# Attention and mixture-of-experts block: the heads' sums through DRAM instead of a TensorE selection product

## The reference

```
x = x + cross_attention(layernorm(x), ctx, ctx, lengths)   # 8 heads of 16 rows
x = x + moe(layernorm(x))                                  # 8 experts, top 2, gated SiLU

attention, per batch and head (16 rows q, k = v, 512 columns each):
    p   = softmax(s * q^T k)          # over the 512 keys
    out = v p^T                       # 16 rows x 512 queries
```

## Time and profile before

| | |
|---|---|
| median of 3 runs | 1163.27 us (1161.13 to 1163.48) |
| profiled execution | 1159.15 us, span 1157.6 us |
| PE busy | 1032.1 us (89%) |
| DVE busy | 684.7 us (59%) |
| ACT busy | 427.0 us (37%) |
| POOL busy | 629.3 us (54%) |
| attention slots with all parts running | about 77 to 499 us of the span |

### The profile page before, as it was taken

One profiled execution on the slowest core, in us unless ns is written; L12 is line 12 of the kernel. 1 busy time (PEld: TensorE's weight loads), 2 busy tenths in 40 slices (PEclk: granted clock), 3 DMA queues, 4 the chain that ended last, 5 costly groups with the idle time before them and its releaser, 6 DMA issues.

```text
span 1157.6 us, 19040 instructions
## 1 busy us (share of the span) xinstructions
PE 1032.1 (89%) x5098; PEld 413.6 (36%) x5099; DVE 684.7 (59%) x1029; ACT 427.0 (37%) x751; POOL 629.3 (54%) x603
## 2 busy tenths in 40 slices
PE   2899999999999999833999999999999999999970
PEld 0223333333333333211444444444444444444430
DVE  5877777777777777114556545455564555534345
ACT  8277777777777777721111111101011110111110
POOL 5455666666666652321677618348381574800575
PEclk9999999999999999976999999999999999999995
DMA  6575666656665542104878737647585576743779
GB/s 181 184 223 174 187 191 194 190 188 190 193 191 187 176 150 71 45 29 119 236 187 214 227 86 218 174 111 206 147 228 160 149 192 167 200 91 74 158 197 281
DMA packets 213752, 195.86 MB, mean 169 GB/s; under 512 B 138400, under 2 KB 177312, under 8 KB 208288
## 3 DMA queue, kind: packets, MB, share of 16 engines
q1 hardware_dynamic: 198784, 122.27, 40.0%
q0 software_dynamic: 14336, 71.87, 18.8%
q10 hardware_dynamic: 576, 1.05, 0.3%
HBM read 111.48 MB, written 53.00 MB: 142 GB/s over the span
## 4 chain that ended last, share of the span: by engine, by line
PE 77%; DVE 10%; DMA 5%; issue 4%; ACT 1%; POOL 1%; POOLq 1%; SPq 0%; DVEq 0%
PE rows L1169 32%; PE heads_out L1169 16%; PE heads_out L1083 8%; PE scores L1070 8%; DVE nm L768 8%; PE rows L1056 7%; PE misc L1133 2%; PE misc L1110 1%; ACT W L650 1%; DVE st L878 1%; PE misc L1125 1%; DMA sums_dram<-U 1%; PE misc L1103 1%; DMA slots_dram<-cv 0%; PE misc L1149 0%
## 5 line engine op out<-in xcount | busy, mean ns | idle before, releaser
L1169 PE MATMUL rows<-W,U 128*128 (+1 forms) x1776 | 391.5, 380 | 18.3 <-DMA U<-stage 16.9
L768 DVE TENSOR_REDUCE nm<-rows 128x2 f32<-128x1024 f32 x256 | 305.1, 1215 | 80.9 <-PE rows L1056 72.6
L650 ACT ACTIVATE W<-scores 128x512 f32<-128x512 f32 x512 | 284.0, 596 | 124.9 <-PE scores L1070 123.6
L1169 PEld LDWEIGHTS rows<-W,U 128*128 128x128 bf16 x1776 | 174.2, 98 | 229.6 <-issue 22.4
L715 ACT ACTIVATE U<-rows 128x512 f32<-128x512 f32 x78 | 46.3, 597 | 507.8 <-PE rows L1169 492.1
L1169 PE MATMUL heads_out<-W,U 128*128 x888 | 199.4, 381 | 3.3 <-DMA U<-U 3.3
L974 DVE TENSOR_TENSOR U<-rows,U 128x512 bf16<-128x512 f32 x78 | 53.9, 691 | 228.6 <-ACT U L715 228.4
L1056 PE MATMUL rows<-W,U 96*128 96x512 bf16 x512 | 148.5, 400 | 36.3 <-DMA W<-parts_dram 22.5
L434 POOL TENSOR_TENSOR W<-U,W 128x2048 bf16<-128x2048 f32 x42 | 171.4, 4080 | 7.7 <-POOL W L433 7.7
L1070 PE MATMUL scores<-U,W 128*128 128x512 bf16 x512 | 167.7, 384 | 5.9 <-ACT W L650 5.2
L433 POOL TENSOR_SCALAR W<-U 128x2048 bf16<-128x2048 f32 x42 | 80.8, 1924 | 147.0 <-PE rows L1169 139.9
(11 more groups left out here) (169 smaller groups left out, 689.3 us busy)
## 6 DMA issues: line engine op xcount, KB each, us to landing
U<-wpack_dram POOLq DMA_DIRECT2D x42, 1024.0 KB, 5.9
parts_dram<-U SPq DMA_DIRECT2D x32, 384.0 KB, 4.4
U<-parts_dram SPq DMA_DIRECT2D x64, 192.0 KB, 3.4
W<-parts_dram SPq DMA_DIRECT2D x64, 192.0 KB, 4.3
stage<-slots_dram SPq DMA_DIRECT2D x39, 257.0 KB, 3.0
expert_out_dram<-U SPq DMA_DIRECT2D x39, 256.0 KB
parts_dram<-U SPq DMA_DIRECT2D x32, 256.0 KB, 4.4
stage<-wpack_dram POOLq DMA_DIRECT2D x12, 512.0 KB, 4.7
```

What stands on the lines that cost most here:

```text
L650: s.activation(probs[:, w % 2, j, kk, :], sc[u % 2][:, :], ACT.Exp) \
L768: v.tensor_reduce(nm[:, bb.parity, 2 * k:2 * k + 2], p1[k % 2][:, :].rearrange("p (c k) -> p c k", c=2), AX_X, ALU.max, negate=True).then_ ...
L1169: ins = m.matmul(bank, part_of(s_part, k), W[:, bass.ds(at_w, 512)], start=(k == 0 and n == 0), stop=(k == n_chunks - 1 and n == 2))
```

## The change

The two selection products, the matrices `selu`, and ACT's copy of their result go. Instead all 128 rows of each `og` group are stored to `heads_dram`: group 0 by SP in the batch's own slot, after the load of `rb` and before the store of the maxima; group 1 in the next slot, where the sums were stored. `den` is read from the rows of sums in `heads_dram`, and `us` is loaded by one DMA that picks the 16 rows of each head. ACT's `take_out` now waits for the store of the same group of the batch before. SP now waits there for `z_ready` and `x1_kept` of the batch before, and for `og_ready` in a second place.

```diff
             def slot(b):
@@ sync
                 if behind:
                     sp.wait_ge(S["og_ready"], b.n * 2)
+                    store_heads(pv, 1)
+                    heads = heads_dram[bass.ds(pv.n, 1)].rearrange("o g (j r) q -> (o g j) r q", r=32)
                     for g in range(2):
-                        sp.dma_start(sums_dram[bass.ds(pv.n, 1), 4 * g:4 * g + 4].rearrange("o h q -> (o h) q"),
-                                     og[16:113:32, g, :]).then_inc(S["sums_out"], 16)
-                    sp.wait_ge(S["sums_out"], b.n * 32)
-                    sp.dma_start(den[:, :], sums_dram[bass.ds(pv.n, 1)].rearrange("o h (p f) -> (o h p) f", f=32)) \
+                        sp.wait_ge(heads_out[g], b.n * 16)
+                        sp.nop().then_inc(S["sp_held"], 1)
+                    sp.dma_start(den[:, :], heads[:, DH, :].rearrange("h (p f) -> h p f", f=32)) \
                         .then_inc(S["den_in"], 16)
+                    if b.within(2, B):
+                        sp.wait_ge(S["z_ready"], b.n - 1)
+                        sp.nop().then_inc(S["sp_held"], 1)
+                        sp.wait_ge(S["x1_kept"], b.n - 1)
+                        sp.nop().then_inc(S["sp_held"], 1)
+                    sp.dma_start(us[:, :], heads[:, 0:DH, :]).then_inc(S["us_in"], 16)
...
+                if b.within(0, B - 1):
+                    sp.wait_ge(S["og_ready"], b.n * 2 + 1)
+                    sp.nop().then_inc(S["sp_held"], 1)
+                    store_heads(b, 0)
                 if nb.within(0, B - 1):
                     sp.wait_ge(S["m_ready"], b.n + 2)
@@ sync, new
+            def store_heads(b, g):
+                sp.dma_start(heads_dram[bass.ds(b.n, 1), g].rearrange("o p q -> (o p) q"), og[:, g, :]) \
+                    .then_inc(heads_out[g], 16)
@@ gpsimd
-                g.memset(selu[:, :, :], 0.0).then_inc(k, 1)
...
-                    g.affine_select(out=v, in_=v, compare_op=ALU.not_equal, fill=1.0, base=128 * gr,
-                                    pattern=[[-32, H], [-1, DH]], channel_multiplier=1).then_inc(c, 1)
...
-                    hold(S["us_ready"], b.n)
+                    hold(S["us_in"], b.n * 16)
@@ scalar
-                        act.wait_ge(S["u_ready"], bb.n)
-                        act.wait_ge(S["sums_out"], bb.n * 32)
+                        act.wait_ge(heads_out[gr], bb.n * 16)
...
-                if pv.within(0, B - 1):
-                    act.wait_ge(S["u_ready"], b.n)
-                    if pv.within(1, B - 1):
-                        act.wait_ge(S["z_ready"], b.n - 1)
-                        s.nop().then_inc(S["act_held"], 1)
-                        act.wait_ge(S["x1_kept"], b.n - 1)
-                    s.activation(us[:, :], misc[:, :], ACT.Copy).then_inc(S["us_ready"], 1)
@@ tensor
-                        if (w, u) == (1, 2) and behind:
-                            if reader:
-                                pe.wait_ge(*reader)
-                            pe.wait_ge(S["og_ready"], b.n * 2)
-                            for gr in range(2):
-                                ins = m.matmul(misc[:, :], selu[:, gr, :], og[:, gr, :], start=(gr == 0),
-                                               stop=(gr == 1))
-                            ins.then_inc(S["u_ready"], 1)
-                            reader = (S["us_ready"], b.n)
```

More of the change, by code:

```diff
@@ L90, in build @@
     ys = nc.dram_tensor("expert_out_dram", [T * P, D], F32, kind="Internal").ap()
-    sums_dram = nc.dram_tensor("sums_dram", [B, H, L], F32, kind="Internal").ap()
+    heads_dram = nc.dram_tensor("heads_dram", [B, 2, P, L], F32, kind="Internal").ap()
     recips_dram = nc.dram_tensor("recips_dram", [B, H, L], F32, kind="Internal").ap()
@@ L131, in build @@
         zt = sb("zt", [P, KD, P], F32)
-        selu = sb("selu", [P, 2, P], F32)
         den = sb("den", [P, 32], F32)
@@ L201, in build @@
             prep_steps keys_steps first_keys first_scale first_steps z_steps route_a_steps route_b_steps queries_out keys_out
-            sums_out rec_out m_out den_in rec_in m_in cv_in p1_ready p1_used scores_ready exp_done pv_done
-            og_ready vt_ps vt_ready u_ready us_ready t_ready x1_ready x1_kept zt_ps zt_ready
+            rec_out m_out den_in rec_in m_in cv_in p1_ready p1_used scores_ready exp_done pv_done
+            og_ready vt_ps vt_ready us_in t_ready x1_ready x1_kept zt_ps zt_ready
             gate_ready gate_used mask_ready rank_ready rank_used idx_ready rec_ready st1_steps
@@ L211, in build @@
         st_in = [[sem(f"stack{i}{j}") for j in range(4)] for i in range(2)]
+        heads_out = [sem(f"heads_out{i}") for i in range(2)]
         slots_out = [sem(f"slots_out{i}") for i in range(2)]
@@ L227, in gathered @@
             return in_w[:, b] if b < 12 else in_u[:, b - 12]
-        N_CONST = 9
+        N_CONST = 7
         block = cx.enter_context(nc.Block())
@@ L413, in constants @@
                 g.memset(ident[:, :], 0.0).then_inc(k, 1)
[L414 removed]
                 g.memset(ltri[:, :], 1.0).then_inc(k, 1)
                 g.memset(vt, 0.0).then_inc(k, 1)
[L417 removed]
+                hold(k, 3)
                 g.affine_select(out=ident[:, :], in_=ident[:, :], compare_op=ALU.not_equal, fill=1.0, base=0,
                                 pattern=[[-1, P]], channel_multiplier=1).then_inc(c, 1)
[L420 to L423 removed]
                 g.affine_select(out=ltri[:, :], in_=ltri[:, :], compare_op=ALU.is_gt, fill=0.0, base=0,
@@ L1090, in slot @@
                     (S["rank_used"], b.n - 2) if b.within(B + 1, B + 1) else \
-                    (S["us_ready"], b.n - 1) if b.within(B, B) else None
+                    None
                 for w in range(4):
@@ L1100, in slot @@
                             pe.wait_ge(S["z_ready"], b.n - 1)
-                            pe.wait_ge(*reader)
+                            if reader:
+                                pe.wait_ge(*reader)
                             for k in range(KD):
@@ L1127, in slot @@
                             reader = (S["vt_ready"], b.n + 2)
-                        if (w, u) == (1, 2) and behind:
+                        if (w, u) == (1, 6) and pv2.within(0, B - 1):
                             if reader:
                                 pe.wait_ge(*reader)
-                            pe.wait_ge(S["og_ready"], b.n * 2)
-                            for gr in range(2):
-                                ins = m.matmul(misc[:, :], selu[:, gr, :], og[:, gr, :], start=(gr == 0),
-                                               stop=(gr == 1))
-                            ins.then_inc(S["u_ready"], 1)
-                            reader = (S["us_ready"], b.n)
-                        if (w, u) == (1, 6) and pv2.within(0, B - 1):
-                            pe.wait_ge(*reader)
                             pe.wait_ge(S["mask_ready"], b.n - 1)
```

2 lines of the change are left out of this document (removed).

## The result

The changed kernel took 1190.18 us (median of 4 runs, 1179.58 to 1196.88), against 1162.20 for the kernel before (4 runs, 1159.82 to 1163.48): a ratio of 1.0258, with a 95% interval of 1.023 to 1.0286. The forecast was 1150.4, with a range to 1167. It is slower, and far outside the range. The profiled execution took 1190.37 us.

A forecast was written before the change was run, and what follows sets the result against it. TensorE held 77% of the chain, with DVE pacing part of each slot. 13 slots at 1.0 us, plus 1.7, less 1.0 and 0.8, gave 12.9 us off 1163.27: 1150.4 us, range 1145 to 1167.

The forecast's parts named there:

- PE's 1.72 us and the ceiling of 1.1 per slot: Regular slots: PE loses the 1.72 us product, but DVE then sets the pace, so at most 1.1 us is gained.
- X: Time from issue to landing of group 1's 256 KB store, SP waiting for it: taken as 3.0 us, bounds 2.5 and 5.3.
- the store lands late: Rival, chance 0.19: at SP's wait for group 1's store, from X = 4.7 later DMAs slip; at 5.3, 12 us slower, 1175.
- the second in the list of chains: SP's queue: load of `us` takes 0.5 us of issue; the last query part behind it lands 2.5 to 3 us after issue.
- It stays where it was, within 0.4 us: The reload, next stack's DMA on SP: held by query parts up to 257.8, against 257.88 before; room 0.4 us.
- `rb` at 260 to 260.9: SP's load behind the reciprocals and the reload: issued at 260 to 260.9, against 260.85 before.
- the room of 0.55 to 1.7 us of `x1_ready`: POOL's sum that DVE waits for, behind `rb`: the chain allows a slot shorter by 0.55 to 1.7 us.
- Slots 15 and 1: Slot 15, without maxima, gains 1.7 us; slot 1, with crowded queues, gains nothing and loses 1.0 us to the larger store.
- The tail: Batch 15's chain of sums' store, `den`, reciprocals, `rb`: heads' store takes 3.0 us instead of 2.2, 0.8 us lost.
- The load of `us` lands while the reciprocals travel: In the tail: the load's transfer overlaps the reciprocals' trip; no time was charged for it.

The follow-up runs named there:

- Run 1: Kernel before without the two selection products, ACT copying `og` group 0 to `us`, no DMA added: 1144.38 us, ratio 0.9863, attention ends at 497.7.
- Run 5: Changed kernel without the load of `us`, ACT copying `og` group 0 instead; stores and SP's wait stay: 1148.14 us, ratio 0.9926 to the kernel before.
- run 8: Run 5 with the load of stored heads (8 blocks of 16 rows) put back at its place into an unread tile: 1192.42 us, ratio 1.0325.
- run 9: Run 8 with the unread load reading one group's 128 rows as they lie, 256 KB as well: 1158.41 us, ratio 0.9993 to the kernel before.
- run 17: Changed kernel with sums on their old way, load of `us` behind the query parts and picking 16 blocks of 8 rows: 1150.82 us, ratio 0.9919.
- run 11: Changed kernel with DVE's small mask operation one reduction later: 1202.78 us, ratio 1.0374 to the kernel before.
- run 15: Changed kernel, load of `us` reading group 1's 128 rows as they lie (wrong rows, routing changes): attention ends at 517.5; 1147.39 us, ratio 0.9843.
- run 3: Changed kernel with the load of `us` moved from ahead of the query parts to just ahead of `rb`: 1172.30 us, ratio 1.0088 to the kernel before.

## Why the prediction was wrong

**PE's 1.72 us and the ceiling of 1.1 per slot: right.** Run 1 gave 14.8 us at the end of attention. PE was busy for 25.53 us in the good slot, where 25.4 was to show.

**X: right in kind, too long in size.** It was 2.1 us and not 3.0 in nearly all slots. The 2.6 us that the prediction took from the Trainium skill stand in a section on DMAs issued by GpSimd; this store is SP's, and it landed sooner. The rival "the store lands late" has the sign of the result and came nearest to it (1175), but by another mechanism: its place was SP's wait for the store of group 1, and its condition, X over 4.7, was met in no slot of batches 2 to 14, not even in the slot of 265 us (4.3). The chance of 0.19 was on the wrong place. Run 5 keeps wait and stores and ends attention 12.3 of run 1's 14.8 us earlier.

**The step that failed** is the second in the list of chains: "the load of `us` takes SP some 0.5 us of issue", and then "the last of them is issued at 254.8 and lands 2.5 to 3 later". The issue is 0.58 us. But the last of the query parts behind it landed 4.8 to 6.5 us after its issue, in good slots and long ones, and not 2.5 to 3. I priced the load as issue time alone on SP, and its transfer only in the total ("some 2 us of DMA time at 399 GB/s, against ... 11 us idle"). 399 GB/s is the rate of the earlier trace rows, of full DMA engines. This load ran at 187 to 201 GB/s with a share of half, where the two tails show it. Runs 8 and 9 show the price: the unread load in 8 blocks costs 41.5 us at the end of attention, the same bytes in one block 5.1. How exactly the DMAs behind it in the same queue are held up no row shows. The Trainium skill ("DMA: Bandwidth & Descriptors", Why a DMA increments its semaphore by 16 and not by 1) says that the number of DMA engines is the largest one up to 16 that divides the slowest dimension of both patterns; that is 8 for 8 heads of 16 rows, and 16 for the wide load and for run 17. The trace agrees with its shares, 0.52 to 0.57 against 1.07, though it doesn't name the engines. The diff had the 8 in plain sight.

**"It stays where it was, within 0.4 us", the reload: fell with it.** It was to be issued at 257.9, 8.0 us behind the heads' store. In the good slot it is 9.7 behind, in the long one 13.1.

**`rb` at 260 to 260.9, and the room of 0.55 to 1.7 us of `x1_ready`: the room was rightly watched, and overrun.** From `den` at 269.61 to `rb` at 280.38 it is 10.8 us in the long slot and 9.6 in the good one, where the earlier trace rows have 8.8 and run 5, without the load, has 6.2 to 7.7. Here the loss became time.

**The price of an overrun: not thought of.** I had each late chain cost one for one. It cost double: 2.8 us of waiting brought 1.4 us of half clock and, with DVE's mask now beside POOL's splitting of weights, 1.9 us there. DVE's nine waits for `x1` divide like the slots: the two of 0.8 and 1.0 us stand in slots of 28.1 and 28.3, the seven of 1.6 to 2.9 in slots of 29.4 to 33.9. This is why the slots are of two kinds and not all a little longer. That the mask is a part and not the root is argued from the rows; run 11 tried to take it away and got slower.

**Slots 15 and 1.** From the last transposition to ACT's copy of the last group it is 34.3 us, 35.7 before: 1.4 gained, where 1.7 was forecast. In slot 1 the heads' store cost nothing (6.7 us to `den`, 6.6 before); what grew, behind the load of `us`, is the time from `den` to `rb`, 9.3 us and not 5.9 (6.4 in run 5), where 1.0 was the whole price.

**The tail: right sign, wrong place.** 0.8 was the price for X, and 1.7 was lost. X was 2.1, but the reciprocals behind the load in 8 blocks landed 2.9 us after their issue and `rb` followed after 3.0, where before it followed after 1.54. "The load of `us` lands while the reciprocals travel" names the very overlap that did the harm.

What stays open: how much of the harm of a load in 8 blocks is its half share and how much the order in which the DMA engines finish, since no row names an engine; how much POOL's load of weights adds in the long slots, since no run moved it; what the rest of the loss is in run 15; why in the tail of run 17 the reciprocals, issued 0.6 us behind its 16-block load, still held `rb` for 3.2 us (490.58 to 493.75); and whether `rb`, itself read as 8 blocks (alone in that tail it has shares of 0.53 and 0.55 at 188 to 209 GB/s), would gain from another shape, which was not tried.

## What to carry to other kernels

Price a DMA by its shape as well as by its bytes: look at the outermost dimension of both sides; with 8 there the load had half of the rate that 128 or 16 had here. Then price it at the DMAs queued behind it on the same queue, even where nobody waits for the data itself; moving such a load won 1.7% (run 3 against the kernel after), and the wide shape 3.3% (run 9 against run 8). And don't price the overrun of a chain with less than a microsecond of room one for one: here 2.8 us of waiting made a slot 6.1 us longer. Last, look at the transfers of other engines when you move one: POOL's weights came 3.3 to 3.8 us behind the parts before, and beside them in long slots.

## What the runs showed of the hardware that was not expected

- A 256 KB load in 8 blocks of 16 rows ran at 187 to 201 GB/s with a DMA share of 0.52 to 0.57; in 16 blocks of 8 rows a window of it has 0.99 and 361 GB/s. Unread, it lengthened this kernel by 3.3% (run 8 over run 9), the 128 KB behind it in a slot took 4.7 to 6.7 us to land and not 3.4 to 3.7, and in the tail the 16 KB behind it took 2.6, not 1.4.
- DVE's operation of 128x16 on two tiles of SBUF took 2.13 us beside POOL's TENSOR_TENSOR of 2.13 us, and 0.17 alone. The Trainium skill ("SBUF — State Buffer", SBUF: two separate sides) says that DVE and GpSimd share a pair of ports as an exclusive lock, held for the whole instruction, and that a DVE operation with two inputs in SBUF needs it against a GpSimd one that reads SBUF. The trace agrees: both operations end together, and the mean of the mask over 12 slots is 0.94 us in the kernel after, against 0.17 in the kernel before.
- After 3.5 us without a matmul the granted clock went from 1.00 to 0.50 and stayed there for more than 2 us, and steps of 3.91 us took 5.35. It isn't so each time: behind the 3.3 us without a matmul that ended at 473.7 it stayed at 1.00.
- SP needs 0.58 us to issue the load in 8 blocks, 0.38 for the same bytes as they lie, and 3.66 for eight loads of 16 rows.
- A store of 256 KB landed 2.1 us after its issue on a queue that was just draining, 0.6 sooner than the 257 KB of the earlier trace rows.
